# A graph layer on one core: the target list loaded and searched first, and the last output tile's blocks handled in another order

## The reference

```python
h = relu(layernorm(x))                     # x is 1250 x 512
xn = batchnorm(h, norm1_g, norm1_b)
agg = segment_sum(xn[src], dst) / max(deg, 1)        # 20000 edges, dst sorted
conv = relu(agg @ W_conv + b_conv)
q, k, v = h_dense @ Wq, h_dense @ Wk, h_dense @ Wv   # 256 rows, 8 heads of 64
# random-feature attention with proj (256 features), then @ Wo
y = batchnorm(conv + attention + h, norm2_g, norm2_b)
out = x + y
```

## Time and profile before

| | us |
|---|---|
| median of 3 runs | 176.44 |
| lowest and highest | 176.09, 176.51 |
| the profiled execution | 176.07 |
| its span | 174.2 |
| TensorE busy | 165.6 (95%) |
| VectorE busy | 137.9 (79%) |
| ScalarE busy | 89.9 (52%) |
| GpSimd busy | 7.6 (4%) |

### The profile page before, as it was taken

The page is one execution under the profiler, slowest core; times in us unless marked ns, Lnnn a source line. Parts: engine busy times, 40 slices in busy tenths (PEclk is TensorE's granted clock), DMA queues, the critical chain, the costliest instruction groups (busy, mean ns, idle before and its releaser), DMA issues.

```text
span 174.2 us, 3024 instructions
## 1 busy us (share of the span) xinstructions
PE 165.6 (95%) x1131; PEld 108.9 (63%) x1132; DVE 137.9 (79%) x315; ACT 89.9 (52%) x163; POOL 7.6 (4%) x22
## 2 busy tenths in 40 slices
PE   7899999999999999999999999999999999999960
PEld 2388877545545546557777798684464574767940
DVE  2868889989947786999656785975999998597981
ACT  3426999839694779979416164217600505004050
POOL 5037000000000000000000000000000000000000
PEclk9999999999999999999999999999999999999998
DMA  5997970000610000000000000000294014050046
GB/s 186 362 328 185 346 261 0 0 4 0 218 43 0 4 0 0 0 4 2 0 4 0 0 4 0 0 4 4 70 336 186 0 28 119 6 147 0 4 124 172
DMA packets 11884, 13.71 MB, mean 79 GB/s; under 512 B 1458, under 2 KB 6748, under 8 KB 11868
## 3 DMA queue, kind: packets, MB, share of 16 engines
q1 hardware_dynamic: 10476, 12.13, 21.3%
q10 hardware_dynamic: 1072, 1.10, 1.8%
q0 software_dynamic: 320, 0.26, 0.7%
HBM read 10.92 MB, written 2.56 MB: 77 GB/s over the span
## 4 chain that ended last, share of the span: by engine, by line
PE 88%; DVE 3%; ACT 3%; DMA 2%; issue 1%; DVEq 0%; ACTq 0%
PE bank L978 24%; PE bank L708 20%; PE bank L638 8%; PE bank L659 4%; PE bank L732 4%; PE bank L722 4%; PE bank L751 4%; PE bank L685 4%; PE bank L650 3%; PE bank L630 3%; PE bank L1005 2%; PE bank L696 2%; DMA xs<-in_x 2%; DVE gl L1222 1%; DVE st L1054 1%
## 5 line engine op out<-in xcount | busy, mean ns | idle before, releaser
L978 PE MATMUL bank<-r,gh 128*128 128x512 f16 (+8 forms) x140 | 39.3, 314 | 0.0
L978 PE MATMUL bank<-r,gl 128*128 128x512 f16 (+8 forms) x140 | 39.3, 313 | 0.0
L708 PE MATMUL bank<-wc,xs 128*128 128x512 f32 (+1 forms) x80 | 38.5, 608 | 0.2 <-DVE gl L1222 0.2
L1085 DVE TENSOR_TENSOR ohb<-iota,bcol 128x1280 f16<-128x1280 f16 x25 | 20.5, 818 | 3.7 <-PE bank L650 3.7
L708 PEld LDWEIGHTS bank<-wc,xs 128*128 128x128 f32 (+1 forms) x80 | 13.6, 187 | 11.6 <-issue 11.6
L392 ACT ACTIVATE r<-bank 128x500 f16<-128x500 f32 x25 | 18.3, 764 | 3.4 <-PE bank L650 3.4
L978 PEld LDWEIGHTS bank<-r,gh 128*128 128x128 f16 (+1 forms) x140 | 13.5, 97 | 8.5 <-issue 0.3
L978 PEld LDWEIGHTS bank<-r,gl 128*128 128x128 f16 (+1 forms) x140 | 13.6, 97 | 8.2
L608 ACT ACTIVATE bw<-mv,epst 128x1 f32<-128x1 f32 x4 | 1.2, 295 | 31.0 <-DVE mv L1385 31.0
L638 PE MATMUL bank<-hT,r 128*128 128x256 f32 x64 | 14.5, 381 | 0.0
L650 PEld LDWEIGHTS bank<-ohv,ohb 128*128 128x128 f16 x250 | 9.7, 98 | 6.7 <-issue 5.3
(11 more groups left out here) (177 smaller groups left out, 267.1 us busy)
## 6 DMA issues: line engine op xcount, KB each, us to landing
xs<-in_x SPq DMA_DIRECT2D x15, 256.0 KB, 4.6
out<-xs SPq DMA_DIRECT2D x7, 256.0 KB
r<-in_L_gnn_Wq SPq DMA_DIRECT2D x1, 1024.0 KB, 7.5
r<-in_L_gnn_Wk SPq DMA_DIRECT2D x1, 1024.0 KB, 5.7
wc<-in_L_gnn_W_conv SPq DMA_DIRECT2D x1, 1024.0 KB, 9.1
wvo<-in_L_gnn_Wv SPq DMA_DIRECT2D x1, 1024.0 KB, 11.2
wvo<-in_L_gnn_Wo SPq DMA_DIRECT2D x1, 1024.0 KB, 5.3
xs<-in_x ACTq DMA_DIRECT2D x3, 256.0 KB, 4.2
```

The source lines that it names most:

```text
L708: last = nc.tensor.matmul(acc[0:n, :], xnT[:, f, i * P:i * P + n], wc[:, f, :], start=(f == 0), stop=(f == FT - 1))
L978: last = nc.tensor.matmul(acc[:, 0:cn], gg[0:n, s, f * P:(f + 1) * P], A16[0:n, s, c0:c0 + cn], start=(s == 0 and gg is gh), stop=(s == NT ...
L1085: last = V.tensor_tensor(oh[:, s0:s0 + n, :].rearrange("p s (m t) -> p s m t", t=2), iota16[:, 0:size].rearrange("p (m t) -> p m t", t=2). ...
```

## The change

- Loads: the target list is ScalarE's first transfer, in the place of x tile 1, which is SyncE's second. SyncE waits for x tile 7, not 9, before Wk.
- Search: VectorE waits for the list at its start. The comparison is cut into blocks 0 to 2 (ahead of the first statistics), 3 and 4 (behind them), and 5 to 9 (behind the coefficients). TensorE sums the first five blocks between rousing products, the others after the transposes, into columns of the same bank; VectorE adds the two sums.
- Tile 1 of h: VectorE applies the norm (`normal_second`) and copies the bank with the relu (`store_second`); ScalarE did both.
- Rousing: 15, then 1 after the first half of the search, none later.
- Tail: in f = 2, TensorE's blocks come in the order 2, 0, 1. In f = 3, VectorE scales block 0 and ScalarE blocks 1 (in two halves) and 2. x of block 1 is put into the bank by one product with the identity, 512 columns wide, opened before block 0's transposes; four products add `yT` to it, and ScalarE copies the result. VectorE finishes blocks 0 and 2.

```diff
@@ -41,7 +41,8 @@
-ROUSE, ROUSE_MORE = 18, 3
+SEARCHED = 5
+ROUSE, ROUSE_LATE = 15, 1
...
@@ -116,7 +117,7 @@
-        first = sb("first", [P, 2], F32)
+        first = sb("first", [P, 4], F32)
...
@@ -188,7 +189,7 @@
-        order = [("hT", 0), ("hT", 1), ("first",), ("q", 0), ("q", 1), ("hT", 2), ("hT", 3), ("hT", 4), ("hT", 5),
+        order = [("first",), ("hT", 0), ("hT", 1), ("q", 0), ("q", 1), ("hT", 2), ("hT", 3), ("hT", 4), ("hT", 5),
...
@@ -199,8 +200,8 @@
-        order_end += [("agg", FT - 1, c) for c in range(len(LAST_CHUNKS))] + [("zT", FT - 2, j) for j in (1, 2, 0)]
-        order_end += [("zT", FT - 1, j) for j in range(3)]
+        order_end += [("agg", FT - 1, c) for c in range(len(LAST_CHUNKS))] + [("zT", FT - 2, j) for j in (2, 0, 1)]
+        order_end += [("zT", FT - 1, j) for j in (1, 0, 2)]
...
@@ -310,7 +312,7 @@
-            sp.dma_start(edst[:, :], dst.rearrange("(p j) -> p j", p=EP)).then_inc(dst_in, 16)
+            load_x(1)
...
@@ -320,7 +322,7 @@
-            sp.wait_ge(x_in[NT - 1], 16)
+            sp.wait_ge(x_in[7], 16)
...
@@ -419,16 +421,15 @@
-            for i in (1, 3, 5):
+            act.dma_start(edst[:, :], dst.rearrange("(p j) -> p j", p=EP)).then_inc(dst_in, 16)
+            for i in (3, 5):
-            ln_tile(1)
-            store_hT(1)
...
@@ -609,9 +610,10 @@
-                for a, b in ((0, 512), (512, 1024), (1024, N)) if f < FT - 1 else ((0, 256), (256, 512), (1024, N)):
+                for a, b in ((0, 512), (512, 1024), (1024, N)) if f < FT - 1 else ((512, 768), (768, 1024), (1024, N)):
+            copy_turned(FT - 1, 1)
...
@@ -624,7 +626,10 @@
-                pe.wait_ge(h_ready, i + 1)
+                if i == 1:
+                    pe.wait_ge(n1_ready, 1)
+                else:
+                    pe.wait_ge(h_ready, max(i, 1))
...
@@ -789,14 +794,19 @@
-            def edge_search():
-                pe.wait_ge(nb_ready, 1)
-                acc = pe_open(pe, "first")
+            def edge_search(half):
+                pe.wait_ge(nb_ready, half + 2)
+                if half == 0:
+                    pe_open(pe, "first")
+                acc = bank[uses[("first",)][0]]
+                a, b = ((0, SEARCHED), (SEARCHED, EJ // GR))[half]
-                    for j in range(EJ // GR):
-                        last = nc.tensor.matmul(acc[0:GROWS, hf:hf + 1], below[:, j, hf * GROWS:(hf + 1) * GROWS],
-                                                cone[0:EP, 0:1], start=(j == 0), stop=(j == EJ // GR - 1))
-                last.then_inc(full("first"), 1)
+                    for j in range(a, b):
+                        last = nc.tensor.matmul(acc[0:GROWS, 2 * half + hf:2 * half + hf + 1],
+                                                below[:, j, hf * GROWS:(hf + 1) * GROWS], cone[0:EP, 0:1],
+                                                start=(j == a), stop=(j == b - 1))
+                if half:
+                    last.then_inc(full("first"), 1)
...
@@ -843,11 +853,12 @@
+            edge_search(0)
+            rouse(ROUSE_LATE)
-            edge_search()
-            rouse(ROUSE_MORE)
+            edge_search(1)
...
@@ -994,13 +1005,13 @@
-                    elif j == 1:
+                    elif j == 0:
-                        if f == FT - 1 and i in (0, 2):
-                            pe.wait_ge(z_act, 3 * f + i // 2 + 1)
+                        if f == FT - 1 and i in (4, 6):
+                            pe.wait_ge(z_act, 3 * f + i // 2 - 1)
...
@@ -1021,9 +1032,22 @@
-            transpose_z(FT - 2, (1, 2))
+            transpose_z(FT - 2, (2,))
-            transpose_z(FT - 1)
+            transpose_z(FT - 2, (1,))
+            f = FT - 1
+            c = slice(f * P, (f + 1) * P)
+            acc = pe_open(pe, "zT", f, 1)
+            nc.tensor.matmul(acc[:, 0:512], ident[:, :], xs[:, 4:8, c], start=True, stop=False)
+            transpose_z(f, (0,))
+            for i in range(4, 8):
+                if i in (4, 6):
+                    pe.wait_ge(z_act, 3 * f + i // 2 - 1)
+                o = (i - 4) * P
+                last = nc.tensor.matmul(acc[:, o:o + P], yT[:, f, i * P:(i + 1) * P], ident[:, :],
+                                        start=False, stop=(i == 7))
+            last.then_inc(full("zT", f, 1), 1)
+            transpose_z(f, (2,))
...
@@ -1087,11 +1111,22 @@
+            def normal_second():
+                dve.wait_ge(ln_ready, 1)
+                V.tensor_scalar(xs[:, 1, :], xs[:, 1, :], lnw[:, 2, 1:2], lnw[:, 3, 1:2], ALU.mult, ALU.add).then_inc(n1_ready, 1)
+
+            def store_second():
+                acc = landed(dve, "hT", 1)
+                V.tensor_scalar(hT[:, :, P:2 * P], acc[:, :].rearrange("p (t n) -> p t n", t=FT), 0.0, None, ALU.max
+                                ).then_inc(read("hT", 1), 1)
+
-                V.tensor_scalar(first[0:GROWS, :], acc[0:GROWS, 0:2], -1.0, 0.0, ALU.add, ALU.max).then_inc(read("first"), 1)
+                V.tensor_copy(first[0:GROWS, :], acc[0:GROWS, 0:4]).then_inc(read("first"), 1)
-                V.tensor_scalar(rows[0:GROWS, :], first[0:GROWS, :], float(ROW_MAX), None, ALU.min).then_inc(rows_ready, 1)
+                link(V.scalar_tensor_tensor(out=first[0:GROWS, 0:2], in0=first[0:GROWS, 0:2], scalar=-1.0, in1=first[0:GROWS, 2:4],
+                                            op0=ALU.add, op1=ALU.add))
+                V.tensor_scalar(rows[0:GROWS, :], first[0:GROWS, 0:2], 0.0, float(ROW_MAX), ALU.max, ALU.min).then_inc(rows_ready, 1)
...
@@ -1241,12 +1276,10 @@
-            def edge_thresholds():
-                dve.wait_ge(dst_in, 16)
-                link(V.tensor_copy(edst2[:, :, :], edst[:, ::GR].unsqueeze(2).to_broadcast([EP, EJ // GR, 2])))
-                shape = [EP, EJ // GR, NW // 2, 2]
-                V.tensor_tensor(below[:, :, :].rearrange("p j (w t) -> p j w t", t=2),
-                                edst2[:, :, :].unsqueeze(2).to_broadcast(shape),
+            def edge_thresholds(a, b):
+                shape = [EP, b - a, NW // 2, 2]
+                V.tensor_tensor(below[:, a:b, :].rearrange("p j (w t) -> p j w t", t=2),
+                                edst2[:, a:b, :].unsqueeze(2).to_broadcast(shape),
...
@@ -1254,9 +1287,15 @@
+            dve.wait_ge(dst_in, 16)
+            link(V.tensor_copy(edst2[:, :, :], edst[:, ::GR].unsqueeze(2).to_broadcast([EP, EJ // GR, 2])))
+            edge_thresholds(0, 3)
+            edge_thresholds(3, SEARCHED)
-            edge_thresholds()
+            normal_second()
+            edge_thresholds(SEARCHED, EJ // GR)
+            store_second()
...
@@ -1426,11 +1465,11 @@
-                V.tensor_scalar(yT[:, f, 512:1024], yT[:, f, 512:1024], s2[:, f:f + 1], t2[:, f:f + 1],
+                V.tensor_scalar(yT[:, f, 0:512], yT[:, f, 0:512], s2[:, f:f + 1], t2[:, f:f + 1],
-                for j in range(3):
-                    finish(f, j)
+                finish(f, 0)
+                finish(f, 2)
```

More of the change, by code:

```diff
@@ L261, in gnn_kernel @@
         h_ready = sem("h_ready")
+        n1_ready = sem("n1_ready")
         rows_ready = sem("rows_ready")
```

## The result

Median of 20 runs 176.55 us (176.25 to 179.50), against 176.16 (175.76 to 177.24, 20 runs) for the kernel before on the same chip: ratio 1.0035, interval 1.002 to 1.005 (it is taken over the fast executions, without the one of 179.50, and is not the quotient of the two medians, which is 1.0022). The change makes the kernel slower by 0.39, where 0.7 faster was forecast. The profiled execution took 176.28, its span 174.5 (before: 176.07 and 174.2). Over the runs the median span went from 174.3 to 174.5, and the median time outside the span from 1.88 to 2.11. So about half of the 0.39 is inside the span and half outside it, of which the working had said nothing. The profiled execution shows only the first half: outside its span it has 1.8, and before 1.9.

A forecast was written before the change was run, and what follows sets the result against it. TensorE, busy 95% of the span, was taken as the bound, so savings count only at head and tail. Head 0.4 plus tail 0.3 is 0.7, taking the median from 176.44 to 175.7; range 175.0 to 176.9.

The forecast's parts named there:

- Head, start of the layer norm: VectorE's wait for the target list: first statistics at 4.59, 0.52 late; coefficients at 7.48 instead of 6.96.
- D: Landing time of the target list, taken as 3.9, with bounds 3.56 and 4.96.
- rival (3): Head: the list lands late and holds VectorE up; 176.1 at a landing of 4.3, 176.8 at 4.96; chance 0.30.
- Head, from the coefficients to the next VectorE work: VectorE gains 0.51 after the coefficients, so group 1's statistics start where they did.
- L + 3.16: When VectorE starts group 1's statistics, L being when the norm's coefficients are finished; before the change L + 3.67.
- Head, TensorE: Query products start 0.8 earlier, but k 0 waits for the copy of q 1's bank, so 0.38 is kept.
- Wq is no limit: Head: Wq lands at 9.1, ahead of the query products' start at 10.2.
- it was there in time: Wk was there for k 0 at 20.03, and its earlier issue covers the 0.4 by which k 0 moves.
- Clock: TensorE's clock still rises with five fewer rousing products: cost 0.
- the fourth rival: TensorE's clock falls between the rousing and the query products: 1.0 slower, 177.4; chance 0.10.
- Tail: Stores go out 0.5 to 1.0 earlier, but bandwidth bounds them: saves 0.3, between 0 and 0.8.
- what goes is the hole: Tail: the saving is the gap of about 0.3 in DMA transfers, at 170.1 to 170.5, ahead of the last stores.

The follow-up runs named there:

- e2: Only the head of the change, with the tail of the kernel before: 177.25 us, ratio 1.0065 to the kernel before.
- e5: The changed kernel plus ten one-column TensorE products after the last rousing product: 176.28 us, ratio 1.001 to the kernel before.
- e9: e5 with five rousing products instead of one behind the first half of the search, and six one-column products instead of ten: 176.42 us, ratio 1.0009.
- e10: e5 with its own loads, but VectorE takes the statistics ahead of the list: 176.24 us, ratio 0.9999 to the kernel before.
- e1: Only the tail of the change, on the kernel before: 176.32 us, ratio 1.0001 to the kernel before.
- e6: e4 plus ten one-column TensorE products: 175.73 us, ratio 0.9981 to the kernel before.
- e12: e1 plus ten one-column TensorE products behind the first rousing: 176.70 us, ratio 1.0024 to the kernel before.
- e13: e7 with the tail of the kernel before: 175.34 us, ratio 0.9957 to the kernel before.
- e14: The kernel before with SyncE waiting for x tile 7, not 9, before Wk: 176.18 us, ratio 1.0004.
- e4: The changed kernel with the loads of before and VectorE taking the first two tiles' statistics ahead of the list: 176.39 us, ratio 1.0001 to the kernel before.
- e7: e6 with the copy of q 1's bank moved between the statistics and coefficients of group 2: 175.31 us, ratio 0.9952 to the kernel before.
- e8: The kernel before without its three rousing products behind the search: 176.07 us, ratio 0.9996.
- e15: e1 with SyncE waiting for x tile 7, not 9, before Wk: 176.22 us, ratio 0.9996 to the kernel before.

## Why the prediction was wrong

**Head, start of the layer norm: this step failed, in one term.** D was taken as 3.9. It was 4.58 in the changed kernel, and with the same load of the list 4.15 (e2), 3.97 (e5), 4.60 (e9) and, by the trace's landings, 4.65 (e10, where nobody waited for it): mean 4.39. All else in the step held: bn_stats came 0.70 after the list's landing (0.69 forecast), the coefficients 3.58 after it (3.58). So rival (3) came true in the head: it has a head that brings nothing at D = 4.3 and loses 0.3 at 4.6, and k 0 came 0.40 later with D at 4.58. The error was to put the list 0.15 below x's first tile because it is smaller. By the landings in the five traces the list came 0.25 to 0.35 behind that tile, which was issued at the same time on the other queue (3.69 and 3.97 in e5, 4.40 and 4.65 in e10); and x's second tile, in the list's very place in the kernel before, landed at 4.25. The list's small size bought nothing. By the rule of the Trainium skill ("DMA: Bandwidth & Descriptors", "Why a DMA increments its semaphore by 16 and not by 1") a transfer of 125 rows runs on five engines, from which the prediction read a late landing. The traces agree on the number: five completions stand for the list as one transfer, and 29 (16 and 13) for it as 112 rows and 13. The direction was right too, but as two transfers it landed at 4.24 and 4.19, inside the spread of the single one, and no run shows that the number of engines is the cause.

**Head, from the coefficients to the next VectorE work: right, with a second limit missed.** L + 3.16 gives 11.32; it was 11.31. But x's third tile can be missing: in e5 group 1 began at 10.98, 0.28 after L + 3.16. So in such an execution even the forecast's D would not have brought the forecast's gain. The row at 10.63 has no idle time with a transfer named, and it was rightly read as room: in that trace the tile landed at 9.78. But over the 17 traces it lands between 9.78 and 11.47, and it held VectorE up in kernels with the loads of before too (e1, e6, e12, e13, e14); one profile couldn't show that.

**Head, TensorE: the mechanism was right.** e4, e7 and e8 show the bank of q 1 as the cap: query products 0.9 earlier give 0.4 at k 0, 0.67 of rousing gives 0.30 there, and moving the copy alone took the span from 173.85 to 173.45. From the copy's end to k 0 it takes 0.14, not 0.05. In the changed kernel itself no gap stood there: TensorE had work until 20.32, as long as the copy took (20.28), since both were late by the list. "Wq is no limit" was wrong where the rest is early: in e13 it landed at 10.01, not 9.1, and ended the wait before the query products. Of Wk, "it was there in time" held for the profile read, not for e1's and e12's, which have the same head; the earlier issue is worth something in those executions (e15).

**Clock: perhaps the fourth rival, in a part of the executions.** No profiled execution fell into it, so where the clock fell, and whether its fall or something else made them long, is not shown; that only kernels with the list in ScalarE's first place have such executions in number (16 of 80), and that none came with five full-width products between search and transposes (e9), speaks for the place that the rival named. Without these executions the median of the changed kernel is 176.43 and not 176.55.

**Tail: the hole goes, its worth failed, about 0.1 for 0.3.** The rule "what goes is the hole" took bytes for the bound to the very end. In the profiles the end keeps its distance from the last store's issue, behind the last ready block, and that moved by 0.11; so the prediction's other end, "0 if the hole only moves", was near. The prediction had it move by 0.5 to 1.0, through a term mis-sized: block 1's products with the residual already in the bank were put at 0.4 (168.28 to 168.7), as four transposes, and took 1.06 (L1047, four products in eight records). ScalarE's copy of block 1 therefore ended at 170.47, 2.84 after the scaling and not 2.2 (169.3 less 167.12). The price stood in the prediction itself: the turn with x takes 1.80 for eight products (each listed twice), 0.22 each, where a transpose takes 0.11. Four at 0.22 are 0.9. The wide product likewise took 1.02 for 0.45, but in the gap, where it cost nothing.

**The sum.** Median spans give +0.2, which is a tail of about -0.1 and a head of about +0.3; outside the span +0.23. Together 0.43, against 0.39 measured. The part outside was in no term: the working counted instructions by their time alone, and not by what a shorter program of TensorE does to the fetch of its last block. That 176.55 lies in the stated range, which took in most of rival (3), is in part luck: about half of the loss came from outside the span, of which no rival spoke.

## What to carry to other kernels

A new first link of the critical chain is priced by the landing of that very transfer, over several executions; the landing of another one in its place is off by more than the gain can be. Before saving on an engine, list everything that its next stage waits for with its own time (bank, data, weights): here the copy of q 1's bank, x's third tile, Wq and Wk each came last in some profile, and most was paid only when the copy moved together with the start of the query products (175.31). At the end, ask what the last transfer waits for; a hole ahead of it can be filled and the span end hardly sooner.

## What was unexpected of the hardware

- The same first transfer, nothing ahead of it in its queue, landed between 3.97 and 4.65 in five profiles (after, e2, e5, e9, e10), and each time behind x's first tile, which has three times its bytes.
- A block of instructions fetched behind the last instruction can lengthen the execution: 2.11 outside the span in the changed kernel and 2.18 in e4, at worst 3.25 and 3.44; with 20 more instructions of TensorE 1.90 and 1.88. Fewer instructions made a slower kernel. In the changed kernel's own profile such a fetch cost nothing.
- The three kernels with the head of before and the changed tail (e1, e12, e15) have 2.00 to 2.05 outside; before (that head, the other tail) has 1.88, and e6 (that tail, another head) 1.88 too. It isn't a fetch that the profiles show; it stays open.
- e9 and the clock: granted clock over the span 0.993 or more in all 12 with five products 512 columns wide in the gap, below 0.99 and a long span in 16 of 80 executions with one.
- TensorE stands idle for 0.33 to 0.92 ahead of the aggregation, in 17 profiles of kernels that do the same there, with no releaser in the trace; it stays open.
